# Transposed attention scores: masking by GpSimd selects on the exponentials instead of mask matmuls

## The chip, the cores and the metric

The kernel runs on one core of a Trainium2 chip. Its engines work side by side, each through its own queue in order: TensorE (PE, matmuls; PEld, its weight loads), VectorE (DVE), ScalarE (ACT), GpSimd (POOL), and SyncE (SP), which here only issues DMAs. They wait for each other through semaphores. The metric is the device time of one execution in microseconds, smaller is better.

## The reference

Four stages: causal attention with rotary positions, a mixture of experts with a shared one, a gated convolution and scan block, and the mixture again, each on the layer norm of the running x. The change touches only the attention of the first stage:

```python
B, N, D = (4, 512, 128); H = 16; HD = D // H; SCALE = 1.0 / HD; NEG = -10000.0
q = _rope(q)
k = _rope(k)
add_mask = jnp.where(i[:, None] >= i[None, :], 0.0, NEG).astype(x.dtype)
scores = jnp.einsum('bhqd,bhkd->bhqk', q, k) * SCALE + add_mask
attn = jax.nn.softmax(scores, axis=-1)
out = jnp.einsum('bhqk,bhkd->bhqd', attn, v)
out = out.transpose(0, 2, 1, 3).reshape(b, n, H * HD)
return out @ Wo.T + bo
```

x is 4 x 512 x 128, with 16 heads of 8 features. A query sees the keys up to its own position.

## The kernel before

Attention works on pairs of heads: B = 4 batch entries (a) times HP = 8 pairs (p), PAIRS = 32 pairs, n = 8a + p. The 512 tokens are four blocks of 128 (TT). For every pair the scores are made twice. First `scores` (L942) with queries on the partitions, in three units S0 (blocks 0 and 1), S1 (block 2) and S2 (block 3), from which VectorE's `row_max` (L1379) takes each query's maximum over both heads. `split_max` (L1389) writes the maxima as two bf16 parts into the query table q_tok by three small operations (L1394, L1395, L1397). Then TensorE turns the queries with their maxima (`queries_with_max` L963, by `pair_T`, L929), ScalarE copies them to q2T (L703), and `scores_T` (L968) makes the transposed scores, keys on the partitions, with the maximum already taken off, again in three units T0 (key block 0, 512 queries), T1 (384) and T2 (256 and 128). ScalarE's `exps` (L705) writes their exponentials to probs (two buffers, n % 2). `weigh_values` (L988) multiplies them with the values into one PSUM bank; a column of ones in v_tok gives the sums. After each even pair from 2 on, the two pairs before are copied (`take_weighed`, L713), turned (`weighed_T`, L1008) and divided by VectorE (`divide`, L1399).

The triangle in which a key is later than its query (the reference hides these keys) is a 128 x 128 block in each unit's key or query block. In both kinds of scores it is made negative by added matmuls of a diagonal and a mask table: two in each of two heads, so 16 a pair in `scores_T` (L983), and 16 in `scores` (L958).

PSUM: six of eight banks are a ring of three slots of two banks. `ring_order` (L65) lists the units in the order in which they take slots: S0 and S1 of pair n + 1, T0 of pair n, S2 of pair n + 1, T1, the turned values of even pairs, T2, and the work of the next entry. `give` (L896) waits until the unit three places earlier has been read; `slot_full` and `slot_free` count fills and reads. TensorE's queue (L1041 to L1069) keeps the same order, with the turn of the queries and the weighing of pair n - 1 between S1 and T0.

The next batch entry is prepared meanwhile: norm and projections in pairs p = 0 and 1, then GpSimd's `rope` (L547 to L588) in one run, from the time ScalarE has copied qk_sb (L723) in p = 1. At p = 5 and 6 TensorE turns the new keys and queries (`pre_T`, L933; the first waits for `roped`), and ScalarE (L733) and VectorE (L1375) copy them out. GpSimd also adds the bias rows (`add_bias`, L532), takes inverse roots (L512), and after the rope of entry 1 makes one `partition_all_reduce` (L600). VectorE spreads weight pieces over pairs 0 to 7 (`find_tops`) and 12 to 27 (`take_low_weights`), ScalarE over 11 to 26 (L746).

Of the kernel before, what the change touches and what calls it, by code (L numbers as in the profile page):

```python
# [6 lines left out]
ALU = mybir.AluOpType  # L7
# [170 lines left out]
def hybrid_block_kernel(nc, x_in, wqkv_in, wo_in, bo_in, w1_in, b1_in, w2_in, b2_in, wg_in, gate_rows_in,  # L178
# [3 lines left out]
    with ExitStack() as ctx:  # L182
# [197 lines left out]
        pv_made = sem("pv_made")  # L380
        weighed_ready = sem("weighed_ready")
# [127 lines left out]
        def _(pool):  # L509
# [37 lines left out]
            def rope(a):  # L547
# [4 lines left out]
                for t in range(TT):  # L552
# [9 lines left out]
                    for to, of in ((even, odd), (odd, even)):  # L562
                        ins = nc.gpsimd.tensor_tensor(s_to[:, :, :, to], qk[:, :, :, of], all_heads(sin, to), ALU.mult)
                link(ins)
                link(nc.gpsimd.tensor_tensor(rope_c[:], rope_c[:], rope_s[:], ALU.add))
                q32, k32 = (rope_c[:, :, k * D:(k + 1) * D].rearrange("p t (h d) -> p t h d", h=H) for k in range(2))
# [13 lines left out]
                link(nc.gpsimd.tensor_copy(k_slot(1), kr))  # L580
                nc.gpsimd.tensor_copy(q_slot(2), q_slot(0))
# [11 lines left out]
            for a in range(1, B):  # L593
                add_bias(a)
                rope(a)
                if a + 1 < B:
                    inverse_root(a + 1)
                if a == 1:
                    pool.wait_ge(tops_found, 1)
                    nc.gpsimd.partition_all_reduce(bounds[:, 0:3], tops[:, 0:3], P,  # L600
                                                   bass.bass_isa.ReduceOp.max).then_inc(bounds_ready, 1)

# [292 lines left out]
        def _(pe):  # L895
# [72 lines left out]
            def scores_T(n, u):  # L968
# [5 lines left out]
                for j in PROB_UNITS[u]:  # L974
                    size = L - P * j
                    for h in range(2):
                        rows = slice(W2 * h, W2 * h + MAX_AT + 2)
                        pe.matmul(ps[:, to + h, o:o + size], kT[rows, a % 2, p, j * P:(j + 1) * P],  # L978
                                  q2T[rows, n % 2, j * P:L], start=True, stop=False)
                    for r in range(2):  # L980
                        for h in range(2):
                            rows = slice(W2 * h, W2 * h + W2)
                            mm = pe.matmul(ps[:, to + h, o:o + P], neg_eye[rows, r, :], mask_kq[rows, r, :],  # L983
                                           start=False, stop=(r == 1))
# [3 lines left out]
            def weigh_values(n):  # L988
# [7 lines left out]
                read_by(("T", n, 2))  # L996
# [44 lines left out]
            for n in range(PAIRS):  # L1041
# [5 lines left out]
                queries_with_max(n)  # L1047
                if n >= 1:
                    weigh_values(n - 1)
                scores_T(n, 0)  # L1050
# [809 lines left out]
```

## Time and profile before

| | |
|---|---|
| median of 3 runs | 800.47 us (799.57 to 800.96) |
| profiled execution | 800.33 us, span of its trace 798.5 us |
| TensorE busy | 566.2 us (71% of the span), 5836 matmuls |
| VectorE busy | 466.9 us (58%) |
| ScalarE busy | 344.6 us (43%) |
| GpSimd busy | 327.8 us (41%) |

The page gives busy time by engine, the chain of work that ended last, and groups of instructions by source line with the idle time ahead of them and who ended it. In the timeline each row has a start, a duration, the engine, the line, written and read tensors with their shapes, and in brackets how long the engine had been idle and on whom it waited. Matmul durations overlap, since they are pipelined: distances are taken from start to start.

### The profile page before, as it was taken

What the parts mean: (1) busy time and instruction counts of PE and PEld (TensorE: products, weight loads), DVE (VectorE), ACT (ScalarE), POOL (GpSimd) and SP (SyncE); (2) the same over time, 40 slices, a digit from 0 to 9 for tenths busy, and PEclk for the clock granted to TensorE, in tenths of its full rate; (3) what the DMA queues carried; (4) which work ended last, traced back from release to release, by engine and by line L of the source; (5) the groups of instructions that cost most, each with busy time, mean ns of one, the idle gap of its engine ahead of it and who ended that gap; (6) DMA issues with size and microseconds to landing.
All of it is one profiled execution on the core that took longest, in us unless ns stands there. A gap on an engine that the chain in (4) does not pass through costs nothing. (4 is left out here: it accounts for less than half of the span.)

```text
span 798.5 us, 16946 instructions
## 1 busy us (share of the span) xinstructions
PE 566.2 (71%) x5836; PEld 377.7 (47%) x5836; DVE 466.9 (58%) x1241; ACT 344.6 (43%) x462; POOL 327.8 (41%) x447
## 2 busy tenths in 40 slices
PE   3488887888888744564888886545777667888870
PEld 2354554545544333342766665122424446666650
DVE  5868767676677354465433443488796763443434
ACT  0254645655665423452444443131524444444430
POOL 5036028018100027765466555112432544566550
PEclk9789999999999957687899999675958768999995
DMA  8999000000000010011211111200000002111105
GB/s 297 321 335 298 2 2 2 2 1 2 2 1 2 1 30 27 18 31 40 56 49 48 45 39 30 77 27 0 28 15 14 27 28 57 48 48 48 38 29 161
DMA packets 45146, 46.37 MB, mean 58 GB/s; under 512 B 5369, under 2 KB 42386, under 8 KB 44810
## 3 DMA queue, kind: packets, MB, share of 16 engines
q1 hardware_dynamic: 40522, 35.91, 15.0%
q0 software_dynamic: 4544, 9.38, 3.6%
q8 instruction: 52, 0.85, 0.5%
q14 instruction: 28, 0.23, 0.1%
HBM read 16.75 MB, written 28.52 MB: 57 GB/s over the span
## 5 line engine op out<-in xcount | busy, mean ns | idle before, releaser
L1384 DVE TENSOR_REDUCE row_maxima<-ps 128x2 f32<-128x256 f32 (+3 forms) x128 | 99.0, 817 | 44.1 <-PE ps L958 43.9
L661 POOL DMA_INDIRECT y_dram<-arena,goes_to x78 | 85.4, 1095 | 82.1 <-DVE arena L1650 73.9
L710 ACT ACTIVATE probs<-ps 128x768 f32<-128x768 f32 (+1 forms) x96 | 82.5, 884 | 81.1 <-PE ps L983 81.1
L831 ACT ACTIVATE arena<-ps,up_back 128x512 f32<-128x512 f32 x78 | 53.6, 688 | 133.5 <-PE ps L1194 133.5
L512 POOL TENSOR_TENSOR rstd<-var_eps,minus_half 128x4 f32<-128x4 f32 x16 | 17.0, 1061 | 220.5 <-DVE var_eps L1321 220.5
L1650 DVE COPY arena<-ps 128x128 f32<-128x128 f32 x78 | 22.8, 292 | 127.4 <-PE ps L1205 127.3
L643 POOL DMA_INDIRECT rows_dram<-probs,idx x64 | 68.9, 1077 | 49.4 <-DVE idx L1582 29.5
L1194 PE MATMUL ps<-arena,w 128*128 128x128 f16 x936 | 87.0, 227 | 0.2
L1205 PE MATMUL ps<-w,probs 128*128 x936 | 85.2, 217 | 1.2 <-DVE probs L1642 0.8
L1003 PE MATMUL ps<-probs,v_tok 128*16 128x256 f32 (+3 forms) x512 | 74.7, 434 | 2.5 <-ACT probs L710 2.5
L1205 PEld LDWEIGHTS ps<-w,probs 128*128 128x128 f16 x936 | 66.5, 96 | 15.9 <-issue 2.7
L1194 PEld LDWEIGHTS ps<-arena,w 128*128 x936 | 65.8, 99 | 12.0 <-issue 1.1
L1642 DVE SCALAR_TENSOR_TENSOR probs<-arena,hid_scale,probs 128x512 f16<-128x512 f32 x78 | 58.8, 753 | 4.2 <-ACT probs L836 3.8
L836 ACT ACTIVATE probs<-arena,hid_scale 128x512 f16<-128x512 f32 x78 | 56.3, 721 | 2.6
L1189 PE MATMUL ps<-which,bias_rows 128*128 128x128 bf16 x312 | 32.3, 227 | 30.7 <-issue 30.7
L1003 PEld LDWEIGHTS ps<-probs,v_tok 128*16 128x16 f32 x512 | 24.2, 96 | 47.7 <-issue 35.6
L953 PE MATMUL ps<-heads_arena 48*128 48x128 bf16 (+3 forms) x256 | 37.8, 310 | 11.6 <-DVE row_maxima L1384 6.3
L978 PE MATMUL ps<-q2T,heads_arena 50*128 50x512 bf16 (+3 forms) x256 | 38.5, 310 | 9.1 <-ACT probs L710 7.1
L1189 PEld LDWEIGHTS ps<-which,bias_rows 128*128 128x128 bf16 x312 | 18.7, 100 | 43.5 <-issue 43.5
L652 POOL TENSOR_SCALAR result_row<-qk_sb,list_end 128x1 f32<-128x1 f32 x78 | 30.4, 390 | 16.4 <-DMA qk_sb<-rows_dram 6.6
L958 PE MATMUL ps<-mask_qk,neg_eye 64*128 64x128 bf16 x512 | 35.1, 222 | 0.0
L1159 PE MATMUL ps<-w,arena 128*128 128x128 f16 x384 | 25.1, 226 | 12.8 <-DVE arena L1616 12.8
(234 smaller groups left out, 1091.3 us busy)
## 6 DMA issues: line engine op xcount, KB each, us to landing
rows_dram<-grids SPq DMA_DIRECT2D x2, 8840.0 KB, 43.7
qk_sb<-rows_dram SPq DMA_DIRECT2D x78, 65.0 KB, 1.8
arena<-in_w SPq DMA_DIRECT2D x2, 2304.0 KB
arena<-y_dram SPq DMA_DIRECT2D x8, 512.0 KB, 4.1
y_dram<-arena,goes_to POOLq DMA_INDIRECT x78, 2.4
x_all<-in_x SPq DMA_DIRECT2D x4, 256.0 KB, 8.1
rows_dram<-probs,idx POOLq DMA_INDIRECT x64, 2.3
out_x<-x_all SPq DMA_DIRECT2D x4, 256.0 KB, 3.7
```

The costliest lines, as they stand in the source:

```text
L643: nc.gpsimd.indirect_dma_start(rows_dram[r].ap(), bass.IndirectOffsetOnAxis(ap=idx[:, r, b, t, k:k + 1], axis=0), xrow_words[:, b % 2, t, ...
L661: nc.gpsimd.indirect_dma_start(y_dram.ap(), bass.IndirectOffsetOnAxis(ap=goes_to[:, n % YT:n % YT + 1], axis=0), y_t[:, n % YT, :], None). ...
L710: nc.scalar.activation(probs[:, n % 2, :, PROB_AT[u]:PROB_AT[u] + size], ps[:, of:of + 2, 0:size], ACT.Exp).then_inc(slot_free[slot_of(("T ...
L831: nc.scalar.activation(hid_t[:, n % HT, :], ps[:, of, :], ACT.Gelu, scale=up_back[:]).then_inc(bank_free[of], 1)
L836: nc.scalar.activation(hid16_t[:, n % HT, 0, :], hid_t[:, n % HT, :], ACT.Identity, scale=hid_scale[:]).then_inc(high_t_ready, 1)
L978: pe.matmul(ps[:, to + h, o:o + size], kT[rows, a % 2, p, j * P:(j + 1) * P], q2T[rows, n % 2, j * P:L], start=True, stop=False)
L1003: mm = pe.matmul(ps[quadrant:quadrant + VW, PV_BANK, j * P:L], v_tok[:, a % 2, j, 2 * p + h, :], probs[:, n % 2, h, at:at + size], start=( ...
L1189: pe.matmul(ps[:, to, c * P:(c + 1) * P], bias_rows[:, c * P:(c + 1) * P], which[:, s:s + 1].broadcast_to([P, P]), start=(c == 0), stop=Fa ...
L1194: mm = pe.matmul(ps[:, to, c * P:(c + 1) * P], w1[:, w, bass.ds(expert[s], 1), c * P:(c + 1) * P].rearrange("p o f -> p (o f)"), xgT[:, (r ...
L1205: mm = pe.matmul(ps[:, to, 0:D], hid16_t[:, n % HT, v, c * P:(c + 1) * P], w2[:, w, bass.ds(expert[s], 1), c, :].rearrange("p o d -> p (o ...
L1384: ins = nc.vector.tensor_reduce(row_maxima[:, t, 2 * p:2 * p + 2], ps[:, of:of + 2, o:o + keys], AX.X, ALU.max)
L1642: nc.vector.scalar_tensor_tensor(hid16_t[:, n % HT, 1, :], hid_t[:, n % HT, :], hid_scale[:], hid16_t[:, n % HT, 0, :], ALU.mult, ALU.subt ...
```

## The change

`scores_T` no longer adds the mask matmuls; its score matmuls open and close their group themselves, so the triangle holds plain scores and their exponentials. GpSimd's new `mask(n)` waits for the exponentials of each unit (ScalarE's `slot_free`) and puts zero where the key is later than the query: one `affine_select` for each of the four key blocks, on 128 partitions x 2 heads x 128 queries of f32, in place in probs. The last one raises `masked`, and `weigh_values` waits for `masked` instead of the last exponentials. GpSimd's queue is now driven pair by pair: `rope` is a generator with stops after two token blocks, after the sum, and after the first low parts; one portion is run in each of p = 2, 3, 4 and 5, ahead of that pair's selects. `add_bias(a + 1)` comes at p = 0, the all-reduce in pair 9 ahead of its selects, the root for entry a + 2 after the selects of p = 7. In TensorE's queue T0 goes ahead of the weighing of pair n - 1. The mask matmuls of `scores` stay.

```diff
@@ -378,6 +378,7 @@
         q2T_ready = sem("q2T_ready")
         pv_cleared = sem("pv_cleared")
         pv_made = sem("pv_made")
+        masked = sem("masked")
         weighed_ready = sem("weighed_ready")
         bias_added = sem("bias_added")
 
@@ -561,8 +562,11 @@
                     nc.gpsimd.tensor_tensor(c_to, qk, all_heads(cos, slice(0, HD)), ALU.mult)
                     for to, of in ((even, odd), (odd, even)):
                         ins = nc.gpsimd.tensor_tensor(s_to[:, :, :, to], qk[:, :, :, of], all_heads(sin, to), ALU.mult)
+                    if t == 1:
+                        yield
                 link(ins)
                 link(nc.gpsimd.tensor_tensor(rope_c[:], rope_c[:], rope_s[:], ALU.add))
+                yield
                 q32, k32 = (rope_c[:, :, k * D:(k + 1) * D].rearrange("p t (h d) -> p t h d", h=H) for k in range(2))
                 qr, kr = (rope_s[:, :, k * D:(k + 1) * D].rearrange("p t (h d) -> p t h d", h=H) for k in range(2))
 
@@ -578,6 +582,7 @@
                 link(nc.gpsimd.tensor_tensor(kr, k32, k_slot(0), ALU.subtract))
                 nc.gpsimd.tensor_copy(q_slot(1), qr)
                 link(nc.gpsimd.tensor_copy(k_slot(1), kr))
+                yield
                 nc.gpsimd.tensor_copy(q_slot(2), q_slot(0))
                 nc.gpsimd.tensor_copy(k_slot(3), k_slot(0))
                 nc.gpsimd.tensor_copy(q_slot(4), q_slot(0))
@@ -590,15 +595,33 @@
             pool.wait_ge(consts_in, 16 * len(attn_loads))
             add_bias(0)
             inverse_root(1)
-            for a in range(1, B):
-                add_bias(a)
-                rope(a)
-                if a + 1 < B:
-                    inverse_root(a + 1)
-                if a == 1:
+
+            def mask(n):
+
+                for u in range(3):
+                    pool.wait_ge(slot_free[slot_of(("T", n, u))], filled(("T", n, u)))
+                    o = PROB_AT[u]
+                    for j in PROB_UNITS[u]:
+                        part = probs[:, n % 2, :, o:o + P]
+                        ins = nc.gpsimd.affine_select(part, part, [[0, 2], [1, P]], ALU.is_ge, 0.0, base=0, channel_multiplier=-1)
+                        o += L - P * j
+                ins.then_inc(masked, 1)
+
+            turning = iter(())
+            for n in range(PAIRS):
+                a, p = divmod(n, HP)
+                if a + 1 < B and p == 0:
+                    add_bias(a + 1)
+                    turning = rope(a + 1)
+                if p in (2, 3, 4, 5):
+                    next(turning, None)
+                if n == HP + 1:
                     pool.wait_ge(tops_found, 1)
                     nc.gpsimd.partition_all_reduce(bounds[:, 0:3], tops[:, 0:3], P,
                                                    bass.bass_isa.ReduceOp.max).then_inc(bounds_ready, 1)
+                mask(n)
+                if p == HP - 1 and a + 2 < B:
+                    inverse_root(a + 2)
 
             norms = [B]
 
@@ -975,13 +998,8 @@
                     size = L - P * j
                     for h in range(2):
                         rows = slice(W2 * h, W2 * h + MAX_AT + 2)
-                        pe.matmul(ps[:, to + h, o:o + size], kT[rows, a % 2, p, j * P:(j + 1) * P],
-                                  q2T[rows, n % 2, j * P:L], start=True, stop=False)
-                    for r in range(2):
-                        for h in range(2):
-                            rows = slice(W2 * h, W2 * h + W2)
-                            mm = pe.matmul(ps[:, to + h, o:o + P], neg_eye[rows, r, :], mask_kq[rows, r, :],
-                                           start=False, stop=(r == 1))
+                        mm = pe.matmul(ps[:, to + h, o:o + size], kT[rows, a % 2, p, j * P:(j + 1) * P],
+                                       q2T[rows, n % 2, j * P:L], start=True, stop=True)
                     o += size
                 mm.then_inc(slot_full[slot_of(("T", n, u))], 1)
 
@@ -993,7 +1011,7 @@
                     pe.wait_ge(pv_cleared, 1)
                 if n >= 2 and n % 2 == 0:
                     pe.wait_ge(weighed_ready, n // 2)
-                read_by(("T", n, 2))
+                pe.wait_ge(masked, n + 1)
                 for u in range(3):
                     at = PROB_AT[u]
                     for j in PROB_UNITS[u]:
@@ -1045,9 +1063,9 @@
                     scores(n + 1, 0)
                     scores(n + 1, 1)
                 queries_with_max(n)
+                scores_T(n, 0)
                 if n >= 1:
                     weigh_values(n - 1)
-                scores_T(n, 0)
                 if after:
                     scores(n + 1, 2)
                 scores_T(n, 1)
```

## Rows read from the trace of the kernel before

**Rows 1.** Groups by line with shapes, 0 to 345 us: busy us, mean ns, idle before.

```profile
L983 PE MATMUL ps<-mask_kq,neg_eye 64*128 64x128 bf16 x512 | 33.1, 221 | 0.0
```

**Rows 2.** Timeline of pair 27: start us, duration us, engine, line.

```profile
246.62 0.40 PE L929 MATMUL ps<-ident,q_tok 128*128 128x128 bf16 x4
...
246.95 2.33 PE L1003 MATMUL ps<-probs,v_tok 128*16 128x512 f32 x16
...
247.06 0.59 ACT L703 COPY q2T<-ps 128x512 bf16<-128x512 bf16 x1 [0.72 <-PE ps L929]
...
249.22 0.39 PE L978 MATMUL ps<-q2T,heads_arena 50*128 50x512 bf16 x2
...
249.56 0.38 PE L953 MATMUL ps<-heads_arena 48*128 48x512 bf16 x2
...
250.09 1.23 DVE L1384 TENSOR_REDUCE row_maxima<-ps 128x2 f32<-128x1024 f32 x1 [0.93 <-PE ps L958]
...
250.84 0.28 PE L978 MATMUL ps<-q2T,heads_arena 50*128 50x256 bf16 x2 [0.51 <-ACT probs L710]
...
251.38 0.23 PE L953 MATMUL ps<-heads_arena 48*128 48x128 bf16 x2
...
251.87 0.18 DVE L1397 CAST q_tok<-max_rest 128x8 bf16<-128x8 f32 x1
...
252.16 0.40 PE L929 MATMUL ps<-ident,q_tok 128*128 128x128 bf16 x4
```

**Rows 3.** Timeline of pair 28, an even one.

```profile
255.09 0.38 PE L953 MATMUL ps<-heads_arena 48*128 48x512 bf16 x2
...
256.94 0.63 PE L1012 MATMUL ps<-ident,weighed 128*128 128x128 f32 x4 [1.07 <-ACT weighed L715]
...
257.89 0.29 DVE L1406 TENSOR_TENSOR att<-ps,rec 128x128 f32<-128x128 f32 x1
...
258.30 0.33 PE L953 MATMUL ps<-heads_arena 48*128 48x384 bf16 x2
...
258.68 0.40 PE L929 MATMUL ps<-ident,q_tok 128*128 128x128 bf16 x4
```

**Rows 4.** TensorE's timeline in pair 8: its scores wait for VectorE.

```profile
103.36 0.39 PE L953 MATMUL ps<-heads_arena 48*128 48x512 bf16 x2 [2.02 <-DVE row_maxima L1384]
```

**Rows 5.** GpSimd's timeline, the rope of batch entry 1.

```profile
54.41 0.73 POOL L561 TENSOR_TENSOR rope_c<-qk_sb,cos 128x256 f32<-128x256 f32 x1 [12.42 <-ACT qk_sb L723]
...
61.04 2.35 POOL L565 TENSOR_TENSOR rope_c<-rope_c,rope_s 128x1024 f32<-128x1024 f32 x1
...
68.29 0.61 POOL L581 COPY q_tok<-q_tok 128x512 bf16<-128x512 bf16 x1
...
72.76 1.16 POOL L588 TENSOR_TENSOR k_tok<-rope_s,k_tok 128x512 bf16<-128x512 f32 x1
```

**Rows 6.** VectorE's and GpSimd's timelines at the same moment.

```profile
67.07 0.62 DVE L1395 TENSOR_TENSOR max_rest<-row_maxima,q_tok 128x8 f32<-128x8 f32 x1
...
67.05 0.61 POOL L579 CAST q_tok<-rope_s 128x512 bf16<-128x512 f32 x1
```

**Rows 7.** TensorE's timeline in pair 5: the turn of its queries, then of new keys.

```profile
75.30 0.40 PE L929 MATMUL ps<-ident,q_tok 128*128 128x128 bf16 x4
...
80.05 1.07 PE L929 MATMUL ps<-ident,k_tok 128*128 128x128 bf16 x16
```

**Rows 8.** GpSimd's timeline round the all-reduce.

```profile
106.59 0.38 POOL L600 PARTITION_ALL_REDUCE bounds<-tops  x1 [5.76 <-issue]
...
114.16 1.25 POOL L534 TENSOR_TENSOR x_all<-x_all,bo 128x512 f32<-128x512 f32 x1 [7.18 <-issue]
```

**Rows 9.** TensorE's timeline, the last weighing of pair 31.

```profile
276.47 2.33 PE L1003 MATMUL ps<-probs,v_tok 128*16 128x512 f32 x16 [1.85 <-ACT probs L710]
```

**Rows 10.** Windows: length, busy PE, PEld, DVE, ACT, POOL, then TensorE's granted clock, DMA.

```profile
36.00:40.00 4.00, 1.87 (x34) 1.07 (x30) 3.79 (x9) 0.00 (x0) 0.00 (x0) 1.00 1.09 334
40.00:44.00 4.00, 3.19 (x33) 1.70 (x32) 3.81 (x8) 2.35 (x3) 1.26 (x1) 0.51 1.10 335
```

## The prediction

> **What bounds the kernel now.** I read the attention stretch first (it runs from about 36 to 285 us), because every edit lies in it; what follows it starts from its end and I let it shift as it is. The groups of instructions by line say that the 512 mask matmuls which go cost 33.1 us of TensorE busy time [rows 1]. Whether that time is on the path is read from the timeline of one head pair. I took pair 27, where GpSimd is idle. Its queries are turned at 246.62 and those of pair 28 at 252.16, so the pair takes 5.54 us [rows 2]. The reader should follow this circle: turn (L929) 0.33, weighing of the pair before (L1003) from 246.95 to 249.22 = 2.27, transposed scores T0 (L978) with their masks 0.34, then S2 (the last score unit of the next pair, L953) at 249.56. VectorE has already been waiting for S2: its reduce of 1.23 starts at 250.09. When that ends (251.32), two things go on: S0 of the pair after takes the ring slot at 251.38, and the maxima are split, ready at 252.05. The next turn starts at 252.16. So from S2's start to the next turn it is 2.60 us, and the waits for exponentials (0.51 before T2, at 250.84) lie in the shade of that reduce. In even pairs there is the turning of the weighed values too (L1012), and the end is S2, reduce, split, division (L1406 ends 258.18), S1 at 258.30, turn at 258.68: 6.52 us for pair 28, 3.59 of them behind S2 [rows 2, 3].
>
> **The change, step by step.**
>
> *T0 moved ahead of the weighing.* Before, ScalarE's copy of the turned queries (247.06 to 247.65) lay under the weighing. Now T0 must wait for it, and TensorE's queue behind T0 holds the weighing, then S2. Times from the turn: copy from 0.44 to 1.03, T0 at 1.09 (0.06 after its releaser, as S0 at 251.38), without masks 0.22 (the next instruction can follow then: half of the 0.34 is about the pair, 0.12 the four masks), weighing from 1.31 to 3.58, S2 at 3.58. It was at 2.94 [rows 2]. In an odd pair the 2.60 behind S2 stay: 0.64 us longer. In an even pair S2 comes equally late; T2 needs S2's slot, so it waits for the reduce (5.34) and is no help; the division ends at 3.58 + 3.09 = 6.67 and the turn follows at 7.1, where it was 6.52: 0.57 longer [rows 3]. This holds for pairs 1 to 30 except 8 and 16: there VectorE is late by itself (S2 waited 2.02 us for its reduces [rows 4]), the shift is hidden, and the masks save perhaps 0.3 each. Sum: 15 x 0.64 + 13 x 0.57 - 0.6 = 16.4 us.
>
> *Mask matmuls removed.* T0's are in the sum (0.12 a pair). Those of T1 and T2 end in the wait for the reduce of S2: nothing gained. If that cover were gone, they are worth what the first rival below counts.
>
> *Four selects a pair on GpSimd.* No row shows a select. From below: a one-input cast of 512 elements takes 0.61, so 256 take 0.31 [rows 6]; from above 0.78, which is two thirds of the 1.16 of a two-input operation of 512 [rows 5]. The select reads one operand like the cast and has a comparison on top, so I take 0.4, nearer to the cast; a pair's four are 1.6. The Trainium skill (GPSIMD Engine Reference, Performance pitfalls for Q7 kernels) gives compare-and-select bodies 2.03 cycles an element, 1.03 unrolled, at 1.2 GHz: an estimate of 0.43 or 0.22 us for 256 elements. By its lower figure the sum below would be some 5 us smaller. The last two selects start after the third exponential (5.9 in an odd pair, 6.6 in an even one) and are done 0.9 later; the weighing that waits for them wants to start 1.31 into the next pair, at 7.5 or 8.4. Outside the rope they are hidden with over 0.7 us to spare.
>
> *Rope in four portions.* From the trace: two token blocks 3.3 (half of 54.41 to 61.04), the other two and the sum 3.3 + 2.35 = 5.7, up to 68.29 another 4.9, the rest to 73.92 5.6 [rows 5]. Each stands ahead of its pair's selects, so for four pairs GpSimd has 19.5 + 4 x 1.6 = 25.9 us of work in about 26.6. Played through from p = 2: portion 1 done by 2.8, selects wait for exponentials, done 0.4 into p = 3; portion 2 and four selects end 1.5 into p = 4 (TensorE wants them at 1.31: 0.2 lost); portion 3 and selects end 0.8 into p = 5; portion 4 ends at 6.4. There TensorE turns the keys (L929 on k_tok) at 4.75 before [rows 7]; by the later reduce it would be at 5.4, now it waits to 6.4: 1.0. Three such stages: 3.6 us.
>
> *GpSimd against VectorE.* With GpSimd busy, the tiny operation L1395 took 0.62 and ended with GpSimd's own 0.61; its like L1397 takes 0.18 with GpSimd idle [rows 2, 6]. The split has three such operations and stands on the circle. Before, three pairs of each rope suffer from it; now there are selects near the split in all pairs, most of them 0.1 beside it (the second select ends as the split starts), and the pairs p = 3 and 4 suffer more. I take 3 us in all; nothing from below, and from above two selects in each of 28 pairs, 22 us.
>
> *The all-reduce.* Round it GpSimd idled 5.8 us before and 7.2 behind, for "issue" [rows 8]. It now stands between the selects of pairs 8 and 9. 5.8 + 0.4 from about 108 end at 114.3, when the exponentials of pair 9 come anyhow; the 7.2 and portion 1 end about 126.2, the selects of pair 10 at 127.8, and TensorE wants them near 128: nothing, up to 4 us if the select waits for the 7.2 too.
>
> *Rest.* ScalarE's copy is now exposed where ScalarE is behind (key copies, weight pieces): an estimate of 1.0 us, some 0.1 in each of ten pairs. Pair 31 ends its exponentials 0.5 earlier (T0 earlier, no masks), and the last weighing, which waited 1.85 us for them [rows 9], waits for 0.9 of selects: 0.4. GpSimd's DMAs, SP's queue, add_bias and the roots keep their order against their users.
>
> Sum: 16.4 + 3.6 + 3.0 + 1.0 + 0.4 = 24.4 us. The profiled execution took 800.33 (span 798.5 and 1.8 around it), 0.14 under the median of the runs, 800.47. Forecast: 800.5 + 24.4, about 824.5 us.
>
> **The rivals.** (1) *TensorE was the bound and its work is what counts.* Then per pair four mask groups of 0.11 to 0.12 go (14.4 us over 32 pairs), and so do the waits of 0.51 in odd pairs and 1.07 in even ones (15 x 1.58 = 23.7), against an exposed copy of 0.76 in 30 pairs (22.8): 15.3 us faster, 785 [rows 2, 3]. It decides if S2's reduce is not what ends the circle. For it: TensorE has the most busy time of all engines. Against it: S0 starts 0.06 us after that reduce, and VectorE had waited 0.93 us for S2 [rows 2]. Chance 0.12. (2) *GpSimd becomes the bound in the rope.* With a select of 0.78 each portion pair carries 1.5 us more, 6 a stage: 15 more us after the slack, and 0.8 at the end: 840. Heavy collisions with the split come to the same region (up to 846). Chance 0.15. (3) *Change of GpSimd code.* The idle 5.8 and 7.2 round the all-reduce [rows 8] look like a price for changing the kind of operation. If the select paid it as well on each change from and to the rope's operations, four pairs of three stages would each hold 13 us more of GpSimd: over 150 us, near 980. In the trace multiplications, casts and the power follow one another without such a gap, so 0.02. The Trainium skill (GPSIMD Engine Reference, Instruction dispatch) tells of about 6 us on the first call into a freshly loaded kernel; the gap of 5.8 agrees with it. (4) *TensorE's clock.* In 40 to 44 us 0.51 of full speed was granted, the lower of its two levels, after TensorE had been busy for 1.87 of the 4 us before [rows 10]. The new idle stretches are 0.7 and 1.1 in a pair and 2.0 at the key turn. If the clock drops there for the 2.3 us of weighing, each time costs about 2; at three key turns it is inside my range, in every pair it would give over 860. Chance 0.04. (5) *No net change*, the late S2 being made good by idle VectorE: 800, chance 0.02; nothing in the rows supports it, since the reduce starts as soon as S2 is there.
>
> **How the numbers follow.** The forecast has 0.65. Its own range is 814 to 834: selects of 0.31 and no collisions take off 6 to 10, 0.6 of slack misjudged in a stage or a wait at the all-reduce adds as much. The range that should hold 8 in 10 reaches into rival 2: 812 to 841. A measurement of this kernel tells about 0.2% (1.6 us) from no change. Slower has the forecast, 2, 3 and 4 (0.86), no change 0.02, faster 0.12.
>
> **What would show it.** Right: in a pair with GpSimd free of rope, TensorE idle 0.7 us before T0 (releaser the query copy), S2 3.6 us behind the turn instead of 2.9, the wait for probs before T2 gone and one for row_maxima in its place, period 6.2 and 7.1. Selects of 0.4. The key turn waits for GpSimd's last k_tok operation by about 1 us in pairs 5, 13 and 21. Attention ends near 309. Wrong: S2 not later; selects over 0.6 with the weighing waiting for them (rival 2); a gap of some 6 us between selects and rope operations (rival 3); granted clock under 0.9 over whole pairs (rival 4).

## The result, and the profile after

The changed kernel takes 825.75 us (825.07 to 832.9, 4 runs) where the kernel before took 800.72 in the same session (799.57 to 801.51, 4 runs): ratio 1.0334 (1.0276 to 1.0392), about 25 us or 3% slower. The run of 832.9 had a mean granted TensorE clock of 0.848, the others 0.859 to 0.863. The profiled execution took 825.67, of which 823.9 are span. The forecast was 824.5, so the total is right. Whether its terms are right is the rest of this text.

All of the loss lies where it was looked for. The last addition to x_all in attention ends at 310.15 (before: 285.13), and from there to the end of the span it is 513.7 us (before: 513.4).

From the page of the kernel after: busy time of the engines, then groups by line (busy us, mean ns, idle time ahead and who ended it).

```profile
PE 570.2 (69%) x5324; PEld 366.4 (44%) x5324; DVE 465.5 (56%) x1241; ACT 348.4 (42%) x462; POOL 376.8 (46%) x575
...
L606 POOL TENSOR_SCALAR_AFFINE_SELECT probs<-probs 128x256 f32<-128x256 f32 x128 | 52.4, 428 | 118.5 <-ACT probs L733 118.1
...
L1021 PE MATMUL ps<-probs,v_tok 128*16 128x256 f32 (+3 forms) x512 | 85.0, 479 | 3.1 <-POOL probs L606 3.1
...
L1001 PE MATMUL ps<-q2T,heads_arena 50*128 50x512 bf16 (+3 forms) x256 | 32.2, 308 | 30.4 <-ACT q2T L726 24.6
```

512 matmuls are gone and TensorE is busy for 4 us more than before (570.2 against 566.2): part of its work now runs at a lower granted clock. GpSimd's 49 us more go with the 52.4 of the selects. The last row is the heart of it: T0 has waited 24.6 us for ScalarE's copy of the turned queries, 32 times 0.77, which was hidden before.

Timeline of the kernel after, pairs 27 and 28 (start us, duration us, engine, line; in brackets the idle time before and its releaser). It answers [rows 2, 3]; L952 is L929 there, L1021 is L1003, L976 is L953, L1001 is L978.

```profile
265.42 0.40 PE L952 MATMUL ps<-ident,q_tok 128*128 128x128 bf16 x4
265.86 0.58 ACT L726 COPY q2T<-ps 128x512 bf16<-128x512 bf16 x1 [0.72 <-PE ps L952]
...
266.59 0.39 PE L1001 MATMUL ps<-q2T,heads_arena 50*128 50x512 bf16 x2 [0.77 <-ACT q2T L726]
...
266.91 2.33 PE L1021 MATMUL ps<-probs,v_tok 128*16 128x512 f32 x16
...
269.17 0.39 PE L976 MATMUL ps<-heads_arena 48*128 48x512 bf16 x2
...
269.72 1.22 DVE L1402 TENSOR_REDUCE row_maxima<-ps 128x2 f32<-128x1024 f32 x1 [1.76 <-PE ps L981]
...
271.00 0.23 PE L976 MATMUL ps<-heads_arena 48*128 48x128 bf16 x2 [0.99 <-DVE row_maxima L1402]
...
271.46 0.77 POOL L606 TENSOR_SCALAR_AFFINE_SELECT probs<-probs 128x256 f32<-128x256 f32 x2 [0.30 <-ACT probs L733]
...
271.50 0.41 DVE L1415 CAST q_tok<-max_rest 128x8 bf16<-128x8 f32 x1
...
271.97 0.40 PE L952 MATMUL ps<-ident,q_tok 128*128 128x128 bf16 x4
...
273.45 4.03 PE L1021 MATMUL ps<-probs,v_tok 128*16 128x512 f32 x16
...
280.83 0.40 PE L952 MATMUL ps<-ident,q_tok 128*128 128x128 bf16 x4
```

Read it from the turn at 265.42. T0 starts 1.17 behind it (forecast 1.09), the weighing at 1.49 (1.31), S2 at 3.75 (3.58; before 2.94). VectorE had waited 0.93 us for S2's scores and now waits 1.76. TensorE's wait for exponentials before T2 is gone and one of 0.99 for row_maxima stands in its place. The next turn comes 6.55 us after the last (before 5.54). New too: the tiny split operation L1415 takes 0.41 beside two selects, where its like took 0.18.

Pair 28 takes 8.86 us. There the same sixteen weighing matmuls take 4.03 us instead of 2.33. The windows of that stretch (length, busy PE, PEld, DVE, ACT, POOL, TensorE's granted clock, the DMA engines' share and GB/s):

```profile
272.00:273.00 1.00, 0.36 (x4) 0.19 (x4) 1.00 (x2) 0.58 (x1) 0.23 (x1) 1.00 0.00 0
273.00:274.00 1.00, 0.87 (x4) 0.24 (x6) 1.00 (x3) 0.44 (x1) 0.00 (x0) 0.83 0.00 0
274.00:277.00 3.00, 3.00 (x12) 0.79 (x10) 0.63 (x1) 0.58 (x1) 0.41 (x1) 0.50 0.00 0
```

Half speed, the lower level of 1.2 GHz, was granted during the weighing itself, after the two idle stretches of 0.99 and 0.77 us ahead of it. Seven of the 32 weighings are lengthened in this way, those in pairs 1, 11, 16, 20, 24 and 28 and the last one; they take 3.59 to 4.03 us each, 10.3 more in all than at 2.33. In the kernel before there is none.

Periods of some pairs, measured from one copy of the turned queries to the next, so that the kernels can be compared (us; t0_portions and one_select are experiments below):

| pair | before | after | one_select | t0_portions |
|---|---|---|---|---|
| 27 (odd, clean) | 5.53 | 6.54 | 6.36 | 6.47 |
| 28 (even, clean) | 6.52 | 8.87 | 7.17 | 7.29 |
| 6, 14, 22 | 9.26 | 9.26 | 9.26 | 9.60 |
| 16 | 10.33 | 9.37 | 9.26 | 10.57 |
| 5 | 8.16 | 9.23 | 9.27 | 9.15 |
| 13, 21 | 7.85, 8.16 | 10.02, 10.02 | 9.66, 9.66 | 9.30, 9.31 |
| 11 | 8.06 | 9.17 | 6.36 | 6.50 |
| 20, 24 | 7.33, 6.66 | 8.82, 8.65 | 8.87, 8.87 | 7.29, 7.29 |

### The profile page after: what moved, and what is told of

It is laid out like the page before. It is cut to its first block and busy times, and to the rows that moved or that the text cites. A ratio compares the mean times of both kernels' runs of the same rounds, so it can differ in the third digit from the quotient of the medians.

```text
span 823.9 us, 16057 instructions
## 1 busy us (share of the span) xinstructions
PE 570.2 (69%) x5324; PEld 366.4 (44%) x5324; DVE 465.5 (56%) x1241; ACT 348.4 (42%) x462; POOL 376.8 (46%) x575
## 5 line engine op out<-in xcount | busy, mean ns | idle before, releaser
L606 POOL TENSOR_SCALAR_AFFINE_SELECT probs<-probs 128x256 f32<-128x256 f32 x128 | 52.4, 428 | 118.5 <-ACT probs L733 118.1
L666 POOL DMA_INDIRECT rows_dram<-probs,idx x64 | 66.6, 1041 | 50.6 <-DVE idx L1600 30.7
L1021 PE MATMUL ps<-probs,v_tok 128*16 128x256 f32 (+3 forms) x512 | 85.0, 479 | 3.1 <-POOL probs L606 3.1
L1001 PE MATMUL ps<-q2T,heads_arena 50*128 50x512 bf16 (+3 forms) x256 | 32.2, 308 | 30.4 <-ACT q2T L726 24.6
L1021 PEld LDWEIGHTS ps<-probs,v_tok 128*16 128x16 f32 x512 | 25.4, 102 | 61.5 <-issue 52.5
L976 PE MATMUL ps<-heads_arena 48*128 48x128 bf16 (+3 forms) x256 | 37.4, 307 | 18.2 <-DVE row_maxima L1402 10.2
L1177 PE MATMUL ps<-w,arena 128*128 128x128 f16 x384 | 27.5, 237 | 12.2 <-DVE arena L1634 12.2
```

The lines of the kernel that those rows point to most:

```text
L606: ins = nc.gpsimd.affine_select(part, part, [[0, 2], [1, P]], ALU.is_ge, 0.0, base=0, channel_multiplier=-1)
L666: nc.gpsimd.indirect_dma_start(rows_dram[r].ap(), bass.IndirectOffsetOnAxis(ap=idx[:, r, b, t, k:k + 1], axis=0), xrow_words[:, b % 2, t, ...
L1021: mm = pe.matmul(ps[quadrant:quadrant + VW, PV_BANK, j * P:L], v_tok[:, a % 2, j, 2 * p + h, :], probs[:, n % 2, h, at:at + size], start=( ...
```

## The experiments

My theory (A) was the prediction's: the late T0 costs some 16 us through S2 and the reduce, the GpSimd part some 8, the removed matmuls nothing. The rivals were that the loss comes from GpSimd (selects, rope portions, collisions; B) and that the idle stretches lower the clock (C). no_masks also tests whether removed TensorE work pays. Each kernel is compared with the kernel before in its own session, whose median went from 800.72 to 807.04. Where a time is set against the changed kernel's 825.75, that is another session; with each kernel's own "before" taken off, weigh_first is 5.7 below the change, one_select 6.4, filler 6.5 and s2_first_selects 10.5.

**t0_first**: the kernel before with T0 ahead of the weighing, nothing else.

```diff
                 queries_with_max(n)
+                scores_T(n, 0)
                 if n >= 1:
                     weigh_values(n - 1)
-                scores_T(n, 0)
```

> The kernel before with one edit: the first unit of transposed scores T0 goes ahead of the weighing of the pair before; mask matmuls stay, GpSimd does what it did. Theory A (the circle through S2: whatever makes S2 later in TensorE's queue is paid in nearly every pair): S2 comes some 0.9 us later after the turn, which odd pairs pay in full and even pairs partly: 814 to 820 us, T0 waiting 0.77 us for the query copy in each pair. Theory B (the 25 us come from GpSimd: selects, rope portions, collisions): within 2 us of the kernel before, 800 to 803. Theory C (the granted clock falls because TensorE has a new idle stretch of 0.77 us): stretches at half clock in weighings, as in pair 28 of the changed kernel, and over 820.

Measured 833.16 (832.09 to 834.65) against 800.93, ratio 1.0397 (1.0375 to 1.042): +32 us, about twice what A expected and more than the whole change. B's 800 to 803 is out; C's "over 820" fits the number. Clean pairs cost what A says (pair 27 6.47, pair 28 7.29), but pairs 2, 3, 18 and 19, in which GpSimd runs the rope in one piece, take 9.5 to 9.9, and 10 and 11 take 10.1 and 9.5. Timeline of t0_first, pair 2:

```profile
63.80 0.17 DVE L1395 TENSOR_TENSOR max_rest<-row_maxima,q_tok 128x8 f32<-128x8 f32 x1
63.80 2.38 POOL L565 TENSOR_TENSOR rope_c<-rope_c,rope_s 128x1024 f32<-128x1024 f32 x1
64.00 2.22 DVE L1397 CAST q_tok<-max_rest 128x8 bf16<-128x8 f32 x1
...
67.13 0.40 PE L929 MATMUL ps<-ident,q_tok 128*128 128x128 bf16 x4
...
69.05 3.54 PE L1003 MATMUL ps<-probs,v_tok 128*16 128x512 f32 x16
```

A cast of 8 elements takes 2.22 us, as long as GpSimd's operation beside it lasts. The split stands on the circle, so the next turn waits; and after that hole the weighing runs at a lower clock (0.57 granted from 68 to 72 us). Six weighings are lengthened here, by 8.2 us in all, so C has a share. So T0's place and the order of GpSimd's work can't be added up from separate prices.

**weigh_first**: the changed kernel with the weighing back ahead of T0 (the diff above the other way round).

> The changed kernel with the weighing of the pair before put back ahead of T0; selects and rope portions stay. Theory A: S2 is back in its place, so most of the loss goes; but the weighing now wants the selects 1.0 us earlier, and in odd pairs they end about 0.6 us after it wants to start: 808 to 815 us, with TensorE waiting for the selects (L606). Theory B: the loss stays, 822 to 830. If both bear half: 812 to 818.

Measured 820.28 (816.47 to 825.79, 5 runs), ratio 1.0236 (1.0218 to 1.0253): 5.5 below the change, above the 808 to 815 of A and a little below the 822 to 830 of B. The late S2 is gone (pair 27 5.52), but TensorE now reaches the weighing before the selects are done. Its waits (us in total, times, longest) and one place in its timeline:

```profile
PE ps L1021 <- POOL probs L606: 17.7, 19, 3.8
```

```profile
128.72 1.49 POOL L606 TENSOR_SCALAR_AFFINE_SELECT probs<-probs 128x256 f32<-128x256 f32 x4
...
130.36 1.04 PE L1021 MATMUL ps<-probs,v_tok 128*16 128x512 f32 x2 [3.83 <-POOL probs L606]
```

The changed kernel waits only 3.1 us there. T0 ahead is thus what gives the selects their time: it trades 17.7 us of waiting for 24.6 us at the copy. The five runs spread over 9 us, and their mean granted clock goes with them: 0.867 at 816.47, then 0.857, 0.852, 0.849, and 0.842 at 825.79. The trace is that of the fastest.

**no_masks**: the kernel before without any mask matmul in the transposed scores.

```diff
-                        pe.matmul(ps[:, to + h, o:o + size], ..., start=True, stop=False)
-                    for r in range(2):
...
-                            mm = pe.matmul(ps[:, to + h, o:o + P], neg_eye[rows, r, :], mask_kq[rows, r, :],
-                                           start=False, stop=(r == 1))
+                        mm = pe.matmul(ps[:, to + h, o:o + size], ..., start=True, stop=True)
```

> The kernel before without the mask matmuls of the transposed scores and without any select, so the exponentials of later keys are not set to zero and the output is that of attention that sees them. It prices the removed work alone. Theory A: T0's masks are on the circle (0.12 us a pair, 3.6 us in all), the others end in the wait for the reduce of S2: 796 to 798 us. Rival (TensorE's work is the bound): 14 us of issue time go, 786 us or less.

Measured 803.28 (801.66 to 805.15, 10 runs) against 800.93, ratio 1.0027 (1.0013 to 1.0041). Neither: taking 33.1 us of TensorE work [rows 1] away made the kernel 0.27% slower. Pair 27 gained 0.11 us, so the work itself was worth little, as A says. But windows of no_masks show where the gain went:

```profile
267.00:271.00 4.00, 2.14 (x24) 1.16 (x23) 2.32 (x6) 3.31 (x5) 0.00 (x0) 1.00 0.00 0
271.00:275.00 4.00, 4.00 (x18) 1.23 (x16) 0.00 (x0) 0.19 (x1) 0.00 (x0) 0.57 0.00 0
```

TensorE was busy for 2.14 of 4 us, and then 0.57 of full speed was granted while it was busy throughout. Its weighings at 270.86 and 277.73 take 4.0 each, where the kernel before has 2.33 [rows 9]; with four earlier ones they are 8.6 us longer in all.

**one_select**: the changed kernel with one select a pair, the last, instead of four.

```diff
-                    for j in PROB_UNITS[u]:
+                    for j in (PROB_UNITS[u] if u == 2 else ()):
+                        if j == 2:
+                            o += L - P * j
+                            continue
```

> The changed kernel with one select a pair (the last key block) instead of four; the triangles of key blocks 0 to 2 are left unmasked. GpSimd loses 1.1 us of work a pair, the queue order of TensorE stays. Theory A: only the wait of the key turn (1.25 us in pair 5), waits for selects in the rope pairs and part of the collisions with the split go: 816 to 822 us. Theory B: the loss is carried by the selects and falls by most of it: 803 to 810.

Measured 819.52 (818.74 to 820.68), ratio 1.0229 (1.0209 to 1.025): 6.2 below the change, in A's range and far from B's 803 to 810. Timeline of one_select at the end of pair 27, beside the 271.50 and 271.97 of the kernel after:

```profile
266.64 0.18 DVE L1418 CAST q_tok<-max_rest 128x8 bf16<-128x8 f32 x1
266.68 0.41 POOL L609 TENSOR_SCALAR_AFFINE_SELECT probs<-probs 128x256 f32<-128x256 f32 x1 [6.52 <-ACT probs L736]
...
266.91 0.40 PE L955 MATMUL ps<-ident,q_tok 128*128 128x128 bf16 x4
```

Without the selects of T1 and the first of T2 the split is undisturbed and the pair is 0.18 shorter. Pair 11 falls from 9.17 to 6.36 and pair 28 from 8.87 to 7.17. These two make 4.5 of the 6.2, and they are not all that A had named: the key turns still wait 4.7 us for GpSimd in all (5.3 in the changed kernel), and in pair 28 it is the weighing that runs at full speed again. TensorE's timeline of one_select at that weighing:

```profile
266.13 0.23 PE L979 MATMUL ps<-heads_arena 48*128 48x128 bf16 x2 [0.99 <-DVE row_maxima L1405]
...
268.08 0.39 PE L1004 MATMUL ps<-q2T,heads_arena 50*128 50x512 bf16 x2 [0.77 <-ACT q2T L729]
268.40 2.33 PE L1024 MATMUL ps<-probs,v_tok 128*16 128x512 f32 x16
```

The same two idle stretches stand ahead of it as in the changed kernel, and here the clock does not fall. So they alone don't decide which weighing is lengthened.

**filler**: the changed kernel with six matmuls ahead of T0, in the time in which TensorE waits for the copy. T0 overwrites their product.

```diff
                 if u == 0:
+                    for r in range(3):
+                        for h in range(2):
+                            rows = slice(W2 * h, W2 * h + MAX_AT)
+                            pe.matmul(ps[:, to + h, 0:384], kT[rows, a % 2, p, 0:P], kT[rows, a % 2, p, P:L],
+                                      start=True, stop=True)
                     pe.wait_ge(q2T_ready, n + 1)
```

> The changed kernel with six more score-sized matmuls (48 rows, 384 columns, their result is overwritten) in TensorE's idle 0.77 us before T0, into T0's own slot; nothing else is changed. Theory C (part of the loss is the granted clock, which falls to its lower level in single weighings such as that of pair 28, 1.7 us each, some four of them in the trace): with TensorE busier these stretches go and the time falls by 3 to 8 us, 818 to 823. Theory A alone: 825 to 827, the matmuls fit into the wait.

Measured 820.56 (817.13 to 822.64), ratio 1.0242 (1.0214 to 1.0269): with more work the kernel is 5.2 us faster, and the two intervals of the ratio just miss each other. Timeline of filler, pair 28:

```profile
267.23 0.40 PE L952 MATMUL ps<-ident,q_tok 128*128 128x128 bf16 x4
267.56 0.66 PE L998 MATMUL ps<-heads_arena 48*128 48x384 bf16 x6
268.30 0.39 PE L1006 MATMUL ps<-q2T,heads_arena 50*128 50x512 bf16 x2
268.62 2.33 PE L1026 MATMUL ps<-probs,v_tok 128*16 128x512 f32 x16
```

The weighing that took 4.03 takes 2.33, and pair 28 7.09 instead of 8.87; pair 24 goes from 8.65 to 7.09, pair 1 from 10.79 to 9.28. The traces of the two kernels are 7.7 us apart at the end of attention (310.15 and 302.49), and these three make 4.9 of it. Pair 11 gives 2.3 more, but there the wait of 0.79 for the selects is gone as well, and pairs 8 and 16 lose 0.8 each. So C holds as a part: some 5 us of the 25 are clock, not order. The traces show how much there is of it (weighings of 2.7 us and more, by the pair in which they stand):

| kernel | lengthened weighings | longer in all |
|---|---|---|
| before, portions | none | 0 |
| t0_portions | 1, 8 | 2.8 |
| after | 1, 11, 16, 20, 24, 28, last | 10.3 |
| one_select | 1, 16, 20, 24, last | 7.7 |
| filler | 20, last | 2.5 |
| no_masks | 1, 4, 9, 12, 31, last | 8.6 |
| t0_first | 1, 3, 4, 11, 19, 20 | 8.2 |

T0 ahead of the weighing brings few of them as long as the mask matmuls stay and the rope is in portions; with the mask matmuls gone there are many. Not all of that time need be on the path: pair 16 has a lengthened weighing and is still shorter than before.

**portions** and **t0_portions**: the kernel before with GpSimd's work in the order of the change, its waits for exponentials included, but no selects and with all mask matmuls; the second also with T0 ahead. Edits against the change:

```diff
             def mask(n):
                 for u in range(3):
                     pool.wait_ge(slot_free[slot_of(("T", n, u))], filled(("T", n, u)))
-                    o = PROB_AT[u]
...
-                ins.then_inc(masked, 1)
```

> The kernel before with one edit: GpSimd's rope runs in four portions, each waiting for the exponentials of the pair before as in the changed kernel, with no selects; mask matmuls stay and the weighing stays ahead of T0. The output is the reference's. Theory A: the rope's operations meet the split at other times, in four pairs instead of three, and the key turn is reached in time: 799 to 804 us. Rival (the portioning itself costs, by late keys): 806 or more.

> The kernel before with T0 ahead of the weighing and the rope in portions, no selects, mask matmuls kept: the changed kernel without its selects and with its masks. T0 alone gave 833 us, because in pairs 2, 3, 18 and 19 single rope operations of up to 2.35 us held up the split that now stands late in the pair. If those collisions are an accident of when the rope runs, portions take most of them away: 820 to 826 us, and then the selects with the removed masks cost nothing on balance (825.75). If portions do not help: 831 to 835, and removed masks are what brought the changed kernel down.

Measured: portions 804.56 (800.62 to 806.25, 10 runs) against 802.43, ratio 1.0026 (1.001 to 1.0042), just above A's range. t0_portions 814.98 (813.57 to 817.03), ratio 1.0157 (1.013 to 1.0183), below both expectations. The rope in portions costs 2.1 alone and saves 18 once T0 is ahead (833.16 to 814.98): its long sum is now behind a wait for exponentials, off the split's time; pairs 2, 3, 11 and 19 give back 2.2, 3.4, 3.0 and 2.8 of it. The steps to the change, by medians, each less its own session's before: 2.1 for the portions, 10.4 for T0 ahead (12.55 in all), 12.5 for selects in place of mask matmuls. By the end of attention in the traces (285.13, 288.98, 301.42, 310.15) they are 3.9, 12.4 and 8.7. The last step is thus the less certain one, and the 7.5 us by which its lengthened weighings exceed those of t0_portions are nearly as long as all of it.

**no_t0_masks**: the kernel before without the four mask matmuls of T0 (the edit of no_masks, for u = 0 only).

> The kernel before without the mask matmuls of T0 only (4 of 16 a pair); the triangle of the first key block stays unmasked, so the output is not the reference's. Leaving out all 16 gave 803.3 us, although pair 27 fell from 5.53 to 5.42: the granted clock was at its lower level for longer. Theory: 0.11 us a pair is gained and TensorE stays as busy as before elsewhere, so 797 to 799. If the clock drops as with all 16 gone: 801 to 804.

Measured 800.0 (796.59 to 803.13, 10 runs) against 802.43, ratio 0.9969 (0.9946 to 0.9992): some 0.3% of gain for the masks that stand on the circle, 0.12 us in pair 27. Between the two expectations, and within its interval nearly nothing.

**s2_early**, **s2_first** and **s2_first_selects**: S2 right behind the turn. If S2 is what ends the circle, it should go first. s2_early keeps the weighing ahead of T0; s2_first has T0 ahead as well; s2_first_selects is the change with that order. The first, the others alike:

```diff
-        order += [("T", n, 0)]
         if after:
             order += [("S", n + 1, 2)]
+        order += [("T", n, 0)]
...
                 queries_with_max(n)
+                if after:
+                    scores(n + 1, 2)
                 if n >= 1:
                     weigh_values(n - 1)
                 scores_T(n, 0)
-                if after:
-                    scores(n + 1, 2)
```

> The kernel before with S2 right behind the turn, but the weighing left ahead of T0. Theory A: the reduce and the split leave the path, but the exponentials of T0 and T1 end later in the pair than the slots are wanted for the next S0 and S1, so ScalarE's chain (copy, weighing, T0 at 3.1, exponentials to 5.4) takes its place at 5.8 us in odd pairs: 798 to 808 us. That would show that T0's place ahead of the weighing is a gain as soon as S2 does not stand behind it.

> The kernel before (mask matmuls, no selects) with S2 moved right behind the turn of the queries, then T0, then the weighing; the ring order follows. Theory A (S2's place sets the circle): S2 starts 0.4 us after the turn instead of 2.9, its reduce and the split end near 4.0, off the path, so collisions of the split with GpSimd cost nothing either; then TensorE's own work (5.2 us) bounds odd pairs at 5.2 to 5.3 instead of 5.54 and even ones at 6.2 instead of 6.52, and the rope pairs gain 0.5 more: 785 to 792 us. Rival (the exposed copy behind the turn is what costs, wherever S2 stands): T0 still waits, 812 or more.

> The changed kernel (selects, rope portions, T0 first) with S2 moved right behind the turn. Theory A: pairs without rope fall to about 5.2 and 6.2 us as in the run with mask matmuls; but four pairs of each rope are then bound by GpSimd (its portion and selects are 4.9, 7.4, 6.5 and 7.3 us against pairs of 5.2 and 6.2), which costs 4 to 8 us a stage: 802 to 815 us. If the selects cost nothing beyond their place: 790.

Measured: s2_early 805.42 (804.58 to 806.1) against 802.0, ratio 1.0042 (1.0028 to 1.0057), within its range. s2_first 810.43 (810.18 to 813.29), ratio 1.0118 (1.0092 to 1.0144), where 785 to 792 was expected. s2_first_selects 816.52 (815.89 to 819.55), ratio 1.018 (1.0162 to 1.0198), above both expectations. From s2_early to s2_first T0 goes ahead of the weighing, and that costs 5.0 us: the expectation that its place there becomes a gain once S2 is out of the way is refuted. Two timelines of s2_first, pair 29 from its turn to the next, and T0 of pair 27:

```profile
269.33 0.40 PE L929 MATMUL ps<-ident,q_tok 128*128 128x128 bf16 x4
...
269.66 0.39 PE L953 MATMUL ps<-heads_arena 48*128 48x512 bf16 x2
...
270.93 2.33 PE L1003 MATMUL ps<-probs,v_tok 128*16 128x512 f32 x16
...
274.94 0.40 PE L929 MATMUL ps<-ident,q_tok 128*128 128x128 bf16 x4
```

```profile
257.71 2.67 DVE L1384 TENSOR_REDUCE row_maxima<-ps 128x2 f32<-128x512 f32 x3
258.44 0.39 PE L978 MATMUL ps<-q2T,heads_arena 50*128 50x512 bf16 x2 [0.90 <-DVE row_maxima L1384]
```

With S2 0.33 behind the turn the pair still takes 5.61 (before 5.59). The circle through S2 is broken, and at once TensorE's own queue, from turn to turn with 0.33 at the copy, fills the same length. And T0 now needs the slot of S0: where VectorE has been kept by weight work it has not read it. T0 waits 0.90 in the second timeline, and that pair takes 6.17 (before 5.53). So S2's lateness is a cost, its earliness no gain. With the selects the order is worth 9 us (825.75 to 816.52): pair 29 takes 5.38, but the pairs with rope lose (pair 13 11.62, after 10.02).

**t0_select**: an attempt at the change's good part: weighing ahead of T0, only T0's masks replaced, by one select a pair, rope in portions. Edits against the change:

```diff
-                for u in range(3):
+                for u in (0,):
...
-                    for r in range(2):
+                    for r in (range(2) if u else ()):
```

> What the other runs point to as the one part of the change that might pay: the kernel before, weighing ahead of T0, T0's 4 mask matmuls replaced by one select a pair on GpSimd (it starts after the first exponential and is ready long before the weighing wants it), T1's and T2's masks kept, rope in portions. The output is the reference's. Leaving out T0's masks gave 2.4 us less than the kernel before of the same chip, portions 2.1 more. Theory: the two add up, 799 to 804 us, within a measurement's reach of the kernel before. Rival: the select collides with the split or the clock falls, 806 or more.

Measured 805.78 (803.21 to 809.16, 12 runs) against 807.04, ratio 0.9989 (0.9972 to 1.0005): not to be told from the kernel before. Of the versions with all masks in place that I ran, none beats it clear of noise.

## Why the prediction was right, and where only its sum was

**T0 ahead of the weighing: mechanism right, sum too big.** The circle is as drawn: T0 waits for the copy, S2 is late, VectorE waits for it, the turn follows. In clean pairs portions to t0_portions is +0.94 (pair 27) and +0.77 (pair 28), even above the 0.64 and 0.57: T0 kept its masks there, its start is 0.08 later than I had it, and the weighing follows it by 0.32, not 0.22. The even pair was also misread: 3.59 behind an S2 at 3.58 is 7.17, so 0.65 longer and not 0.57, and one_select has 7.17. But I summed over 28 pairs, and excepted only pairs 8 and 16, which I let stand still. From portions to t0_portions pairs 6, 14 and 22 lose 0.34 each and not 0.57, pair 5 wins 0.4, and pairs 8 and 16 win 1.8 and 0.5 (11.19 and 11.11 in portions). By medians the term was 10.4, not 16.4; the traces, from the end of attention, give 12.4 (288.98 to 301.42). The 16.4 had T0's masks already taken off (0.12 a pair), and these runs keep them, so on equal terms it was too big by another 2 to 3 us.

**Mask matmuls: right for the order, not for the clock.** In pair 27 nothing is gained from T1 and T2, and 0.11 from T0 (forecast 0.12). Not foreseen: no_masks shows the gain to be eaten by the clock.

**The select: right.** 0.41 alone and 0.43 in the mean for 0.4. Of the two estimates, 0.43 and 0.22, worked out from the cycles that the Trainium skill (GPSIMD Engine Reference, Performance pitfalls for Q7 kernels) gives for compare-and-select bodies, the trace bears out the higher.

**The rope: right in kind.** TensorE's timeline of the kernel after in pair 5, which answers [rows 7], with GpSimd's row of the same time:

```profile
79.40 0.40 PE L952 MATMUL ps<-ident,q_tok 128*128 128x128 bf16 x4
...
85.24 1.05 PE L952 MATMUL ps<-ident,k_tok 128*128 128x128 bf16 x16 [1.25 <-POOL k_tok L593]
```

```profile
83.94 1.15 POOL L593 TENSOR_TENSOR k_tok<-rope_s,k_tok 128x512 bf16<-128x512 f32 x1
```

The key turn waits 1.25, and the three together 5.3 us (longest 2.0), where I had three times 1.0. In portions, with neither selects nor T0 ahead, they wait 4.0, and in t0_portions 1.7. The 0.2 of waiting for selects in the weighing of p = 4 did not come.

**GpSimd against VectorE: the picture was off, the size is not isolated.** I took 3.0 with "most of them 0.1 beside it". In a clean odd pair the second and third selects meet the split and cost 0.18 to 0.19, as one_select shows. It shows this in pairs 7, 15, 23, 27 and 29, 0.9 us together, and nothing in 9, 17 and 25. Pairs 13 and 21 lose 0.7 each on top of t0_portions, half of which one_select gives back.

**The all-reduce: the step that failed.** I let it start at 108. GpSimd's timeline of the kernel after, and TensorE's row of the same time:

```profile
112.84 0.77 POOL L606 TENSOR_SCALAR_AFFINE_SELECT probs<-probs 128x256 f32<-128x256 f32 x2 [0.73 <-ACT probs L733]
120.10 0.38 POOL L620 PARTITION_ALL_REDUCE bounds<-tops  x1 [6.49 <-issue]
120.37 1.57 POOL L606 TENSOR_SCALAR_AFFINE_SELECT probs<-probs 128x256 f32<-128x256 f32 x4
128.94 0.72 POOL L562 TENSOR_TENSOR rope_c<-qk_sb,cos 128x256 f32<-128x256 f32 x1 [7.00 <-ACT probs L733]
...
132.20 1.49 POOL L606 TENSOR_SCALAR_AFFINE_SELECT probs<-probs 128x256 f32<-128x256 f32 x4
```

```profile
133.83 2.53 PE L1021 MATMUL ps<-probs,v_tok 128*16 128x512 f32 x6 [0.79 <-POOL probs L606]
```

The all-reduce stands behind the selects of pair 8, and these behind exponentials at 112.8. So everything comes 6 us later than I had it: the gap of 7.00, then portion 1, and only then the selects of pair 10, wanted by the weighing in pair 11. It waits 0.79 and then runs slowly (six matmuls in 2.53, all sixteen in 3.94): pair 11 lost 2.7 against t0_portions, where I had written nothing, up to 4. So the time of the all-reduce was wrong, and its price is the wait and a fall of the clock that I had not joined to it.

**The tail: too small.** Timeline of the kernel after, against [rows 9]:

```profile
299.41 0.76 POOL L606 TENSOR_SCALAR_AFFINE_SELECT probs<-probs 128x256 f32<-128x256 f32 x2 [0.30 <-ACT probs L733]
300.23 3.78 PE L1021 MATMUL ps<-probs,v_tok 128*16 128x512 f32 x16 [2.27 <-POOL probs L606]
```

The wait grew by 0.4 as forecast, and the weighing after it runs at a lower clock and takes 1.45 more.

**The clock: the rival with a chance of 0.04 came true in part.** Its price of about 2 us a time was near (1.7 in pair 28, 1.3 to 1.7 in the seven); it struck in single weighings, not in every pair, for some 5 us by filler, and my sum had nothing for it. My sum had 8 us for everything besides T0; the runs have 14.6 (2.1 + 12.5), or 12.6 (3.9 + 8.7) by the traces. T0's term had 6 too much, or 4 by the traces. The two errors cancel by luck, and the total is better than its parts deserve. The other rivals fell: removed TensorE work brings no 15 us (no_masks), the loss is not GpSimd's alone (t0_portions loses 12.55 without a select), selects are not 0.78, and no gap stands between selects and the rope's operations outside the all-reduce.

What stays open: the last step, 12.5 us by medians, is not split. The clock's 5, the collisions, the waits and the key turns overlap in it in ways that no run separates, and no run has the selects with the mask matmuls kept, which would price the selects alone. Why the clock falls for one weighing and not for the next, and why it differs from run to run in weigh_first, is not shown. That s2_early and s2_first lose in the pairs in which VectorE has weight work is read from timelines only.

## What to carry to other kernels

An operation that waits on another engine's answer, put ahead of long independent work in an in-order queue, can cost its latency in every round, even if the engine has idle time elsewhere: here it waited 24.6 us in 32 rounds and cost 10 to 12. Work taken from TensorE is worth nothing where another circle closes later, and here it was worth less than nothing, because the clock then fell: look at the granted clock of the stretch before counting it. Before a step is moved to an idle engine, ask which tiny operations of its neighbour stand on the circle at that time, and put the long operations elsewhere: here the order of the rope was worth 18 us, though only once T0 stood ahead of the weighing.

## What the runs showed of the hardware

- Beside one GpSimd operation a VectorE cast of 8 elements, 0.18 us alone, took 2.22 us (t0_first). Beside two selects, 0.77 us together, it took 0.41. The Trainium skill (SBUF — State Buffer, Who interferes with whom) says that where a VectorE instruction wants the ports that it shares with GpSimd, and it names casts among those that can, whoever issues first holds them for the whole instruction and the other blocks. The trace agrees: the cast began at 64.00, after GpSimd's 2.38 at 63.80, and both ended within 0.04 us of each other.
- The select ran right behind the all-reduce; the 7.00 us gap came only before the next multiplication (L562, at 128.94; at the same place 7.33 in weigh_first and 7.18 in filler, for "issue"). Where the all-reduce stood before an addition the gap was 7.18 [rows 8]. Between selects and rope operations otherwise there is none.
- The clock fell for single weighings in the midst of regular work: in pair 28 TensorE had idled 0.99 and 0.77 us shortly before. The same stretches stood ahead of a weighing at full speed in one_select. 0.66 us of overwritten matmuls per pair took the fall away in pair 28 and made the kernel 5.2 us faster, and 512 matmuls less made the kernel before 0.27% slower.
